# Mixture-of-experts stage and gather stage of a four-layer kernel: weights fetched by a register, outputs scattered to token rows

## The reference

```python
xn = layernorm(x)                          # first layer: a linear recurrence on xn, layernorm, added to x
shared = silu(xn @ sg_w.T) * (xn @ su_w.T) @ sd_w.T
scores = sigmoid(xn @ gate_w.T) + gate_bias   # 64 experts in 8 groups; the best 4 groups are kept
topk_w, topk_i = top_k(masked_scores, 6)      # 6 experts for each token
topk_w = topk_w / (topk_w.sum() + 1e-8)
h = silu(x @ eg_w[e].T) * (x @ eu_w[e].T)     # expert e: 256 -> 128 -> 256
routed = sum over the 6 experts e of topk_w[e] * (h @ ed_w[e].T)
# third layer: attention inside each token (16 heads of 64 channels); fourth: gated feed-forward with integer weights
```

## Time and profile before

| what | value |
| --- | --- |
| median of 3 runs | 4280.66 us (4277.24 to 4280.9) |
| profiled execution, its own time | 4279.34 us |
| its span in the profile | 4277.6 us |
| PE busy | 3659.8 us (86%) |
| DVE busy | 3339.0 us (78%) |
| POOL busy | 3559.3 us (83%) |
| ACT busy | 1976.5 us (46%) |
| expert stage | 425 to 870 us |
| gather stage | 870 to 1156 us |
| attention and feed-forward | 1156 us to the end |

### The profile page before, as it was taken

The page is one execution under the profiler, slowest core; times in us unless marked ns, Lnnn a source line. Parts: engine busy times, 40 slices in busy tenths (PEclk is TensorE's granted clock), DMA queues, the critical chain, the costliest instruction groups (busy, mean ns, idle before and its releaser), DMA issues.

```text
span 4277.6 us, 78411 instructions
## 1 busy us (share of the span) xinstructions
PE 3659.8 (86%) x27585; PEld 3249.3 (76%) x27777; DVE 3339.0 (78%) x3764; ACT 1976.5 (46%) x2564; POOL 3559.3 (83%) x1937
## 2 busy tenths in 40 slices
PE   4275999910189999999999999999999999999999
PEld 3143888810078888888888888888888888888888
DVE  8644343446489888899889888898889888899887
ACT  1010333300055555555555555555555555555555
POOL 1675555567599999999999999999999999999997
PEclk8687999955599999999999999999999999999999
DMA  9122999954300000000000000000000000000000
GB/s 367 70 101 70 384 385 385 384 190 127 106 3 5 5 5 5 5 6 6 7 5 5 5 5 5 5 6 5 7 5 5 5 5 5 5 5 6 5 8 5
DMA packets 154902, 291.38 MB, mean 68 GB/s; under 512 B 22608, under 2 KB 116048, under 8 KB 154576
## 3 DMA queue, kind: packets, MB, share of 16 engines
q0 software_dynamic: 38912, 151.04, 9.7%
q1 hardware_dynamic: 115664, 135.80, 9.0%
HBM read 181.77 MB, written 104.99 MB: 67 GB/s over the span
## 4 chain that ended last, share of the span: by engine, by line
POOL 39%; issue 29%; PE 3%; DVE 1%; ACT 0%; POOLq 0%; another core or an unknown queue 0%; ACTq 0%; DVEq 0%
POOL at_s L1109 34%; POOL at_m L1093 2%; POOL at_fall L1089 2%; POOL at_m L1086 1%; PE at_den L1325 1%; PE at_num L1325 1%; PE at_work L1297 0%; DVE at_pv L1225 0%; DVE at_s L1217 0%; POOLq L1108 0%; PE at_work L1302 0%; PE at_misc L1355 0%; ACT at_s L1180 0%; PE at_work L1313 0%
## 5 line engine op out<-in xcount | busy, mean ns | idle before, releaser
L1109 POOL TENSOR_TENSOR at_s<-at_s,at_m 128x2048 f32<-128x2048 f32 (+15 forms) x1024 | 2549.5, 2529 | 115.9 <-DVE at_s L1217 114.6
L1180 ACT ACTIVATE at_s<-at_s 128x2048 f32<-128x2048 f32 (+15 forms) x1024 | 1135.8, 1112 | 1259.2 <-POOL at_s L1109 1253.6
L1217 DVE TENSOR_TENSOR at_s<-at_q,at_kp 128x2048 f32<-128x2048 f32 (+15 forms) x1024 | 1309.2, 1279 | 318.6 <-PE at_den L1325 301.9
L1325 PE MATMUL at_den<-k_ident,at_s 128*128 128x128 f32 x10240 | 1290.8, 273 | 55.4 <-ACT at_s L1180 55.4
L1225 DVE TENSOR_TENSOR at_pv<-at_s,at_vp 128x2048 f32<-128x2048 f32 (+15 forms) x1024 | 1309.7, 1279 | 21.2 <-issue 10.0
L1325 PE MATMUL at_num<-k_ident,at_pv 128*128 128x128 f32 x10240 | 1286.2, 273 | 10.1
L1325 PEld LDWEIGHTS at_num<-k_ident,at_pv 128*128 128x128 f32 x10240 | 1162.2, 141 | 145.4 <-issue 123.1
L1325 PEld LDWEIGHTS at_den<-k_ident,at_s 128*128 128x128 f32 x10240 | 1156.9, 141 | 79.9 <-ACT at_s L1180 61.9
L674 POOL DMA_INDIRECT moe_w<-experts,e_weight_row x256 | 242.1, 946 | 213.5 <-PE moe_yp L701 173.2
L138 POOL DMA_INDIRECT slot_x<-e_xn,e_slot x192 | 209.0, 1088 | 152.1 <-DVE e_slot L358 87.6
L694 PE MATMUL moe_gu<-moe_xT,moe_w 128*128 128x128 f32 x2048 | 274.9, 277 | 13.9 <-DVE moe_xT L737 12.0
(11 more groups left out here) (219 smaller groups left out, 3262.8 us busy)
## 6 DMA issues: line engine op xcount, KB each, us to landing
slot_x<-k_region SPq DMA_DIRECT2D x16, 2048.0 KB, 23.3
moe_x<-slot_x SPq DMA_DIRECT2D x256, 128.0 KB
slot_out<-moe_yo SPq DMA_DIRECT2D x256, 128.0 KB
xT<-cmb_xT SPq DMA_DIRECT2D x33, 128.0 KB, 2.1
at_xT<-xT SPq DMA_DIRECT2D x33, 128.0 KB, 2.0
e_x<-u SPq DMA_DIRECT2D x4, 1024.0 KB, 10.5
moe_w<-experts,e_weight_row POOLq DMA_INDIRECT x256, 6.1
x<-e_x SPq DMA_DIRECT2D x4, 1024.0 KB, 5.6
```

Source lines behind the costliest of these rows:

```text
L1109: nc.gpsimd.tensor_tensor(part(s_all, c), part(s_all, c), by_query(m[h][:], c), ALU.subtract).then_inc(sub_done, 1)
L1180: nc.scalar.activation(part(s_all, c), part(s_all, c), ACT.Exp, scale=C ** -0.5).then_inc(exp_done, 1)
L1217: v.tensor_tensor(part(s_all, c), by_query(q[h][:], c), by_key(kp[:], c), ALU.mult).then_inc(mult_done, 1)
L1325: ins = nc.tensor.matmul(dst[:, b * P:(b + 1) * P], buf[:, at:at + P], k.ident[:], start=(x == 0 and b == 0), stop=False, is_transpose=Tru ...
```

## The change

- A slot row grows from 256 to 268 numbers (`ROW`): the last 12 hold, for each of the token's 6 choices, its slot and what must be added to a slot number to give the token row. DVE writes them into `xn` before the slots are handed out; the zero fill grows with the row.
- Of the 256 blocks, buffer j now works through blocks 32 j to 32 j + 31, one per turn (`STREAM` = 32). There are still 8 buffers and 32 turns.
- SP reads one number per block into a register (`value_load` of `k.fetch`): twice the expert plus a flag that says whether the expert differs from the one that this buffer holds. A plain DMA of the weights is started under the condition of that flag.
- ACT loads x, in pairs: those of buffers 4 to 7 in the same turn (at j = 1 and 2 of its loop), those of buffers 0 to 3 for the next turn (at j = 5 and 6).
- DVE compares each row's six slots with the block's own slot numbers (`find`, twice a turn); POOL turns that into the destination row for each of the 128 rows (seven small instructions for each half turn) and scatters `yo` to `picked`, token by token, with an indirect DMA per block.
- In the gather stage SP loads the six rows of 128 tokens with one plain DMA of 768 KB, into one of 5 buffers. Three of the six are weighted and summed on PE, by diagonal matrices that ACT makes; three stay on DVE, which then adds PE's sum. Groups have 4 tiles, weights are converted in 8 steps between tiles, and ACT stores the transposed tiles.

```diff
-FILLS, ZERO_ROW = 16, 1024
+ROW = D + 2 * TOPK
+STREAM = 32
+FILLS, ZERO_ROW = 16, 4 * ROW
...
+                c.mark(v.tensor_copy(k.xn[:, :, D:D + TOPK], top8[:, :, 0:TOPK]))
+                c.mark(v.tensor_tensor(k.xn[:, :, D + TOPK:ROW], tail_base[:], top8[:, :, 0:TOPK], ALU.subtract))
...
-                v.tensor_scalar(k.weight_row[:], block_of, float(P),
-                                k.iota_p[:, 0:1], ALU.mult, ALU.add).then_inc(widx_done, 1)
+                c(v.tensor_copy(block_expert[:], block_of))
+                c(v.tensor_tensor(fresh[:, 1:], block_expert[:, 1:], block_expert[:, 0:SLOT_BLOCKS - 1],
+                                  ALU.not_equal))
+                c(v.memset(view(fresh[:], [[STREAM, SLOT_BLOCKS // STREAM]]), 1.0))
+                v.scalar_tensor_tensor(out=k.fetch[:], in0=block_expert[:], scalar=2.0, in1=fresh[:],
+                                       op0=ALU.mult, op1=ALU.add).then_inc(widx_done, 1)
...
-    TURNS = SLOT_BLOCKS // RING
+    RING, HALF_RING = SLOT_BLOCKS // STREAM, SLOT_BLOCKS // STREAM // 2
+    TURNS = STREAM
...
-                for b in range(SLOT_BLOCKS):
-                    wait(pool, y_done, b - RING + 1)
-                    pool.indirect_dma_start(w[b % RING][:], None, weights,
-                                            bass.IndirectOffsetOnAxis(ap=k.weight_row[:, b:b + 1], axis=0)
-                                            ).then_inc(w_in[b % RING], 16)
+                c = Chain(pool, pool_step)
+                nc.gpsimd.iota(own[:, 0, :], [[STREAM * P, RING]], base=1, channel_multiplier=1,
+                               allow_small_or_imprecise_dtypes=True).then_inc(numbered, 1)
+                nc.gpsimd.iota(own[:, 1, :], [[STREAM * P, RING]], base=T * TOPK, channel_multiplier=1,
+                               allow_small_or_imprecise_dtypes=True).then_inc(numbered, 1)
+                pool.wait_ge(numbered, 2)
+                for i in range(TURNS):
+                    for h in range(2):
+                        part = slice(h * HALF_RING, (h + 1) * HALF_RING)
+                        pool.wait_ge(hit_done, 2 * i + h + 1)
+                        nc.gpsimd.tensor_tensor(hit[:, part, :], hit[:, part, :], xr[:, part, D + TOPK:ROW], ALU.mult
+                                                ).then_inc(rows_known, 1)
+                        pool.wait_ge(rows_known, 2 * i + h + 1)
+                        c(nc.gpsimd.tensor_tensor(hit[:, part, 0:3], hit[:, part, 0:3], hit[:, part, 3:6], ALU.add))
+                        c.mark(nc.gpsimd.tensor_tensor(found[:, 0, part], hit[:, part, 0], hit[:, part, 1], ALU.add))
+                        c(nc.gpsimd.tensor_tensor(found[:, 1, part], hit[:, part, 2], own[:, 1, part], ALU.add))
+                        c(nc.gpsimd.tensor_tensor(found[:, 0, part], found[:, 0, part], found[:, 1, part], ALU.add))
+                        for j in range(h * HALF_RING, (h + 1) * HALF_RING):
+                            wait(pool, y_out[j], 16 * (i - 1))
+                        c.mark(nc.gpsimd.tensor_copy(row[:, i % 2, part], found[:, 0, part]))
+                        nc.gpsimd.tensor_scalar(own[:, :, part], own[:, :, part], float(P), None, ALU.add
+                                                ).then_inc(hit_free, 1)
+                        c.join()
+                        for j in range(h * HALF_RING, (h + 1) * HALF_RING):
+                            pool.wait_ge(y_ready, done(i, j))
+                            pool.indirect_dma_start(scratch["picked"],
+                                                    bass.IndirectOffsetOnAxis(ap=row[:, i % 2, j:j + 1], axis=0),
+                                                    yo[j][:], None).then_inc(y_out[j], 16)
...
+                def load_x(i, j):
+                    if not isinstance(i, int) or i:
+                        act.wait_ge(turned, done(i, j) - RING)
+                        act.wait_ge(rows_known, i * 2 + (j // HALF_RING - 1))
+                        settle(act, act_settled)
+                    act.dma_start(xr[:, j:j + 1, :], x_rows[:, bass.ds(i + j * STREAM, 1), :]).then_inc(x_in[j], 16)
+
+                def blocks(i, first=False, last=False):
                     for j in range(RING + 1):
                         if j < RING:
                             act.wait_ge(gu_done, done(i, j))
@@ -724,17 +776,40 @@
                             act.wait_ge(y_done, done(i, j - 1))
                             wait(act, y_out[j - 1], i * 16)
                             nc.scalar.copy(yo[j - 1][:], yp[(j - 1) % 2][:]).then_inc(y_ready, 1)
-
-                block_loop(act, blocks)
+                        if j in (1, 2) and not first:
+                            load_x(i, 2 * j + 2)
+                            load_x(i, 2 * j + 3)
+                        if j in (5, 6) and not last:
+                            load_x(i + 1, 2 * j - 10)
+                            load_x(i + 1, 2 * j - 9)
+
+                for j in range(RING):
+                    load_x(0, j)
+                blocks(0, first=True)
+                with act.Fori(1, TURNS - 1) as i:
+                    blocks(i)
+                blocks(TURNS - 1, last=True)
...
+                def find(i, h):
+                    part = slice(h * HALF_RING, (h + 1) * HALF_RING)
+                    if not isinstance(i, int):
+                        dve.wait_ge(hit_free, i * 2 + (h - 1))
+                    nc.vector.tensor_tensor(hit[:, part, :], xr[:, part, D:D + TOPK],
+                                            view(own[:, 0, part], [[1, HALF_RING], [0, TOPK]]), ALU.is_equal
+                                            ).then_inc(hit_done, 1)
...
+                        if j and j % HALF_RING == 0:
+                            find(i, j // HALF_RING - 1)
...
-                def load(i, j):
-                    wait(sp, turned, done(i, j) - RING)
-                    settle(sp, sp_settled)
-                    sp.dma_start(xr[j][:].unsqueeze(1), blocks_of("slot_x")[:, bass.ds(i * RING + j, 1), :]
-                                 ).then_inc(x_in[j], 16)
-
-                def store(i, j):
-                    sp.wait_ge(y_ready, done(i, j))
-                    settle(sp, sp_settled)
-                    sp.dma_start(blocks_of("slot_out")[:, bass.ds(i * RING + j, 1), :], yo[j][:].unsqueeze(1)
-                                 ).then_inc(y_out[j], 16)
-
-                for j in range(RING):
-                    load(0, j)
-                with sp.Fori(1, TURNS) as i:
+                w_rows = io["experts"].rearrange("(e p) d -> p e d", p=P)
+
+                def load_w(i, j):
+                    wait(sp, y_done, done(i, j) - RING)
+                    at = bass.ds(i + j * STREAM, 1)
+                    fetch = sp.value_load(k.fetch[0:1, at], min_val=0, max_val=2 * E - 1)
+                    sp.dma_start(w[j][:].unsqueeze(1), w_rows[:, bass.ds(fetch // 2, 1), :], cond=fetch % 2
+                                 ).then_inc(w_in[j], 16)
...
-        RING, GROUP, LATE = 4, 8, 2
+        RING, TURN_RING, GROUP, LATE, DIAG = 5, 4, 4, 2, 3
+        AFTER = GROUP + LATE + 1
...
-                for n in range(NT):
-                    wait(pool, summed, n - RING + 1)
-                    for j in range(TOPK):
-                        pool.indirect_dma_start(y[n % RING][:, j, :], None, scratch["slot_out"],
-                                                bass.IndirectOffsetOnAxis(ap=k.slot[:, n, j:j + 1], axis=0)
-                                                ).then_inc(y_in[n % RING], 16)
...
+                def own_choices(n):
+                    dve.wait_ge(y_in[n % RING], 16 * (n // RING + 1))
+                    for j in range(DIAG, TOPK):
+                        wait(dve, first_done, n * (TOPK - DIAG) + (j - DIAG))
+                        v.scalar_tensor_tensor(out=k.x[:, n, :], in0=y[n % RING][:, j, :],
+                                               scalar=k.choice_w[:, j, n:n + 1], in1=k.x[:, n, :],
+                                               op0=ALU.mult, op1=ALU.add).then_inc(first_done, 1)
...
+                own_choices(0)
                 for n in range(NT):
-                    dve.wait_ge(y_in[n % RING], 16 * TOPK * (n // RING + 1))
-                    for j in range(TOPK):
-                        ins = v.scalar_tensor_tensor(out=k.x[:, n, :], in0=y[n % RING][:, j, :],
-                                                     scalar=k.choice_w[:, j, n:n + 1], in1=k.x[:, n, :],
-                                                     op0=ALU.mult, op1=ALU.add)
-                        if j < TOPK - 1:
-                            c(ins)
-                    ins.then_inc(summed, 1)
+                    if n + 1 < NT:
+                        own_choices(n + 1)
+                    dve.wait_ge(first_done, (n + 1) * (TOPK - DIAG))
+                    dve.wait_ge(acc_done, n + 1)
```

(26 more changed lines are left out.)

166 lines of the change are left out of this document (98 added, 68 removed).

## The result

The kernel after takes 4273.27 us (median of 20 runs, 4261.77 to 4278.69), the kernel before 4279.73 in the same comparison: a ratio of 0.9983, 95% interval 0.9977 to 0.9989. It is faster, clear of the interval, and inside the forecast range, but by 6.5 us where the forecast was 58. That lies within the 0.2% of no change to which the prediction gave 3%. The profiled execution of after took 4267.74 us, its span is 4266.0.

The account below looks back on a forecast made before the run. PE was taken to bound the expert stage and POOL's issuing the gather stage. 4279.3 + 0.7 (front) + 68 (expert turns) + 7 (end) - 134 (gather) = 4221 us, 1.4% faster; range 4145 to 4280.

Parts of the forecast that it names:

- Attention is 73% of the span and isn't touched.: Attention stage: the change leaves it alone, so its time enters the sum with no change.
- What bounds the kernel now: Expert stage: PE sets it, so relieving the DMA gains nothing. Gather stage: POOL's issuing sets 259 of 285.9 us.
- ACT, landing of x: Expert turn: x of buffer 4, issued behind block 0's output copy, makes PE wait 1.6 us, within 1.2 to 2.1.
- ACT, late silu: Expert turn's end: ACT's four load issues make block 7's silu 0.6 us late, and PE waits; 0 to 0.9.
- Sum of the turn: Expert stage: both ACT delays add 2.2 us in each of 31 turns, +68 us (37 to 93).
- PE's program is the same, so 13.7 us a turn is its floor: Expert stage: PE's unchanged work takes 13.7 us a turn; any gain would have to come from outside PE.
- The end: Behind PE's last expert turn: row computation, four scatters and a landing take 9 to 10 us instead of 2.6, +7.
- POOL: Expert turn: scatters and small instructions take 14.0 us, hidden behind PE's 15.9; upper bound 17.8.
- SP: Expert stage: per block a register read plus 0.68 us for the DMA, hidden while the read is under 1.3 us.
- The gather stage: Without POOL's gathers: tile 5 lands at 36 us, then DVE is the bound; 152 us instead of 285.9, -134.
- rivals 1 and 3: Expert stage: no stall for x, POOL the bound, 4163 us, 20%; or same mechanisms, larger, 4240 to 4280 us, 18%.

Follow-up runs that it names:

- Experiment 1: The kernel after with 96 semaphore increments added at the start of PE's program: 4223.46 us, 0.9871 of before.
- experiment 2: The kernel before with 160 semaphore increments added at the start of PE's program: 4322.69 us, 1.0101 of before.
- 7: After with x loads on SP (weights 0 to 3, all x, weights 4 to 7) and 96 PE semaphore increments: 4447.17 us, 0.9941 of before.
- 8: Same edits as 7, plus gather-stage weight loads issued between tiles, against after: 4448.0 us, 0.9936 of before.
- 11: The kernel of 7 run again in another batch: 4217.83 us, 0.9833 of before.
- 3: After with all x loads moved from ACT to SP, behind each half turn's four weight loads: 4254.35 us, 0.9949 of before.
- 12: After with ACT's x loads for buffers 4 to 7 one block earlier, and 96 PE semaphore increments: 4182.2 us, 0.9766 of before.
- 5: After with x loads on SP, ordered weights 0 to 3, all x, weights 4 to 7: 4496.81 us, 1.005 of before.
- 10: The kernel of 5 run again in another batch: 4261.19 us, 0.9946 of before.
- 6: After with the gather stage's ten weight loads issued between tiles and DVE's weight steps later: 4539.33 us, 1.0147 of before.
- 9: The kernel after, unchanged, run again in another batch: 4274.45 us, 0.9975 of before.

## Why the prediction was right or wrong

**"Attention is 73% of the span and isn't touched."** This is the step that failed. Its program isn't touched, its time is: +41.1 us, put at nothing in the sum. Experiment 1 takes 45 us off after without touching anything else, experiment 2 adds 40.5 to before, and 7, 8 and 11 repeat it with 41 to 43. The cause shown is the number of PE's instructions ahead of the loop. That PE stands for an instruction transfer is supported by all 45 gaps, which end 1.2 to 1.7 us behind one. That it does so because the end of a 16 KB piece falls at a bad distance behind the jump fits both numbers, 96 and 160, which were worked out from pieces of 256 instructions before the runs; but no run varied the number in steps, so that part is argued. Without the 41.1 the profiled execution would have taken 4226.6 us against the 4221 forecast; that it comes so near is in part luck, as the expert stage was 15 us over its forecast and the gather stage 8 under.

**What bounds the kernel now.** Right otherwise: the halved DMA load brought the expert stage nothing, and the gather stage fell with POOL's gathers.

**ACT, landing of x.** Right in mechanism and place. Forecast 1.6 us a turn within 1.2 to 2.1; measured 1.0 to 1.4 at buffer 4. With the other waits it is 1.6 in the mean, the forecast number partly by luck: the step held the x of buffers 5 to 7 to be free ("cost nothing more") and had nothing for the first blocks of the turn, and twelve waits in 30 turns stand there.

**ACT, late silu.** Right: forecast 0.6 more, measured 0.65, from a wait of 0.26 to one of 0.91. ACT doesn't finish each copy before it issues: in the turn shown it starts a copy at 705.12 that takes 0.37 us and begins to issue at 705.35. The lateness hangs on the pairs at j = 5 and 6: with all pairs off ACT the wait fell to the 0.25 of before (3), with only the other two moved it stayed 0.9 (12).

**Sum of the turn.** 2.2 us forecast, 2.5 measured, though the two waits have their forecast size: over the whole stage those for x, without the first, make 48.6 us (forecast 50) where there were none, and those for the last product grew from 8.2 to 27.8 (forecast 19 more). **"PE's program is the same, so 13.7 us a turn is its floor"** is the term that was mis-sized: PE's busy time for the same matmuls grew by 16.4 us. About 3 of them are in the two turns at a clock of 0.90 and 0.91; in a turn at full clock PE is busy for 13.2 to 13.6 us instead of 13.0. The ends of matmuls are modelled in the profile, and why they take longer there was not tested, but the time falls with the waits (425.4 us in 12). **The end** gives another 2: from the last copy (948.18) to the first load of y (960.02) are 11.8 us instead of 9 to 10. A shorter start and fewer waits for the transposed x take some 4 us off again.

**POOL.** Hidden, as forecast: its scatters have a mean of 0.99 us and its small instructions 0.19 to 0.24, and POOL still waits 70.9 us for DVE in 490. **SP.** The read is 0.27 us, hidden. But the step's 0.68 us for the DMA part held for a plain issue alone: read, arithmetic and conditional load together are 9.4 / 8 = 1.2 us a block. Under 2.0 it cost nothing, and it is what defeated experiments 3, 5 and 10.

**The gather stage.** 143.6 against 152, -142.1 against -134: the landing of tile 5 was right to 0.3 us and DVE was the bound behind it; DVE's work there was over-counted by some 8 us.

**The range.** It held the time because it reached to rivals 1 and 3. The measured case is none of them: their turns are not there. So the time fell into the range by luck, at a place (less than 0.2% from no change) to which the list gave 3%, and the attention stage that brought it there was no rival.

**The version that beats both.** Experiment 12, 4182.2 us, 0.9766 of before, is what the change is worth in a batch like the first, once two faults that lie outside its idea are removed: a load one block too late, and the place of a loop.

## What to carry to other kernels

When a change alters the number of instructions of an engine that later runs a loop, compare the loop's time stage by stage, and look for waits put down to "issue" that recur once a pass: here 96 increments were worth 45 us, seven times the net effect of the change. Before loads are moved from one queue to another, add up what the receiving queue issues in a turn, with register reads and arithmetic; if that comes near the turn, move the loads within their own queue instead.

## What the runs showed of the hardware that was not expected

- A gap of 1.5 us (mean) in PE's instruction supply, once in a pass of 195 us, costs about 3 us of such a pass. The granted clock falls behind it (0.66 over 5 us) and two other engines wait in the same ring; which of the two takes how much was not measured. Each of the 45 gaps looked at ends 1.2 to 1.7 us behind a 16 KB transfer of the instruction queue.
- Batches on different chips differ in waits that no semaphore explains: in experiments 5 to 8 the stages ahead of the experts took 150 us more, and the expert stage 648.4 against 533.8 us with the same code (6 and 9), while gather and attention took the same time to 2 us (143.9 and 3166.8 in 5, 143.7 and 3167.1 in 10).
- The same 3072 matmuls of the expert stage keep PE busy for 417.4 us where it hardly waits, and for 433.8 where it stops twice a turn.
- A register read from SBUF on SP takes 0.27 us in the median, a conditional load with it 1.2 us in all, a plain load with a register address 0.6 (4.78 / 8).
